# A state-space stage whose time step is computed in another order

## The reference

```
xc, z = split(u @ m_in_w.T)
xc = silu(conv1d(xc) + conv_b)              # 256 channels
x_dbl = xc @ xproj_w.T                      # 8 + 16 + 16 columns
dt = softplus(x_dbl[:, :8] @ dt_w.T + dt_b) # the time step
Bm, Cm = x_dbl[:, 8:24], x_dbl[:, 24:]
# 16 states: h = exp(dt * A) * h + dt * B * u ;  y = sum over states of h * C
y = (y + xc * Dp) * silu(z)
out = y @ m_out_w.T
```

## Time and profile before

| | us |
|---|---|
| median of three timed runs | 2080.14 |
| profiled execution | 2059.48 |
| its span, first to last instruction | 2057.8 |
| TensorE busy | 1652.5 (80%) |
| VectorE busy | 1350.7 (66%) |
| ScalarE busy | 1003.5 (49%) |
| GpSimd busy | 995.8 (48%) |
| mean granted TensorE clock | 0.837 of full |

### The profile page before, as it was taken

One profiled execution on the slowest core, in us unless ns is written; L12 is line 12 of the kernel. 1 busy time (PEld: TensorE's weight loads), 2 busy tenths in 40 slices (PEclk: granted clock), 3 DMA queues, 4 the chain that ended last, 5 costly groups with the idle time before them and its releaser, 6 DMA issues. The chain is left out here.

```text
span 2057.8 us, 23202 instructions
## 1 busy us (share of the span) xinstructions
PE 1652.5 (80%) x7221; PEld 730.4 (35%) x7221; DVE 1350.7 (66%) x1527; ACT 1003.5 (49%) x1638; POOL 995.8 (48%) x524
## 2 busy tenths in 40 slices
PE   7767788888888888875855957698888889879998
PEld 5221222222222222211454744354444445633333
DVE  3079999999999999999552123566565655384444
ACT  3566666676666776674122523154444445441111
POOL 1169999999999999998441153011111000040000
PEclk8878888888888888877957966599999989989999
DMA  3044344434443433333003221422233330100001
GB/s 140 2 104 104 92 103 103 103 93 103 103 103 95 101 90 88 89 87 91 16 30 103 82 67 50 116 59 56 49 77 79 79 79 4 46 0 0 0 0 41
DMA packets 78636, 145.41 MB, mean 71 GB/s; under 512 B 10214, under 2 KB 40782, under 8 KB 76854
## 3 DMA queue, kind: packets, MB, share of 16 engines
q1 hardware_dynamic: 75350, 134.98, 25.8%
q0 software_dynamic: 3216, 9.51, 1.4%
HBM read 87.27 MB, written 23.53 MB: 54 GB/s over the span
## 5 line engine op out<-in xcount | busy, mean ns | idle before, releaser
L574 POOL TENSOR_TENSOR PR<-H,CS 128x1024 f32<-128x1024 f32 x256 | 599.4, 2359 | 75.1 <-DVE H L550 52.8
L550 DVE TENSOR_TENSOR_SCAN H<-DA,X 128x1024 f32<-128x1024 f32 x192 | 431.1, 2273 | 0.0
L456 PE MATMUL psY<-PR,fold 128*64 128x512 f32 x1024 | 341.0, 766 | 4.9 <-POOL PR L574 4.9
L538 DVE TENSOR_TENSOR X<-DU,psB 128x1024 f32<-128x1024 f32 x192 | 235.8, 1228 | 72.9 <-DMA DU<-ab 56.8
L526 ACT ACTIVATE DA<-DT,negA 128x511 f32<-128x511 f32 x384 | 247.6, 709 | 7.3 <-DMA DT<-W 6.4
L1278 ACT ACTIVATE a_PT<-a_psS 128x512 f32<-128x512 f32 x320 | 181.3, 601 | 138.5 <-PE a_psS L1182 134.6
L1325 DVE TENSOR_REDUCE a_MX<-a_psM 128x1 f32<-128x384 f32 (+3 forms) x352 | 205.0, 635 | 47.0 <-PE a_psM L1197 45.5
L1196 PE MATMUL a_psM<-a_kst,a_qst 72*128 72x512 bf16 (+3 forms) x512 | 147.4, 336 | 28.0 <-DMA a_kst<-scratch_k 17.5
L550 DVE TENSOR_TENSOR_SCAN H<-X,XS 128x1024 f32<-128x1024 f32 x64 | 146.2, 2284 | 30.2 <-ACT X L526 30.2
L585 POOL TENSOR_TENSOR XS<-DU,BS 128x1024 f32<-128x1024 f32 x64 | 151.0, 2360 | 0.0
L436 PE MATMUL psB<-ST,sel 96*128 96x512 bf16 x128 | 60.8, 475 | 106.4 <-DVE X L538 106.4
(11 more groups left out here) (258 smaller groups left out, 2733.0 us busy)
## 6 DMA issues: line engine op xcount, KB each, us to landing
CS<-c_rows SPq DMA_DIRECT2D x128, 256.0 KB, 3.8
DT<-W SPq DMA_DIRECT2D x64, 256.0 KB, 4.3
DU<-ab SPq DMA_DIRECT2D x64, 256.0 KB, 4.4
BS<-c_rows SPq DMA_DIRECT2D x64, 256.0 KB, 5.3
scratch_q<-a_partsq SPq DMA_DIRECT2D x24, 384.0 KB, 3.4
a_qst<-scratch_q SPq DMA_DIRECT2D x8, 1152.0 KB
a_kst<-scratch_k SPq DMA_DIRECT2D x24, 384.0 KB
scratch_k<-a_partsk SPq DMA_DIRECT2D x8, 384.0 KB, 4.4
```

Source lines behind the costliest of these rows:

```text
L456: last = nc.tensor.matmul(psY[h * HP:(h + 1) * HP, n % 2 * T:(n % 2 + 1) * T], fold[:, :], chunk(PR[n % 4], h), start=False, stop=n >= NS - 2)
L538: nc.vector.tensor_tensor(both(X[s % 2][:, :]), DU[p][:, at:at + 2, :], psB[:, :].unsqueeze(1).to_broadcast([P, 2, T]), ALU.mult).then_inc ...
L550: nc.vector.tensor_tensor_scan(H[s % 4][:, :], decay, x, 0.0, ALU.mult, ALU.add).then_inc(scan_done, 1)
L574: nc.gpsimd.tensor_tensor(both(PR[s % 4][:, :]), both(H[s % 4][:, :]), CS[q % 2][:, s // 2 % 2, :].unsqueeze(1).to_broadcast([P, 2, T]), A ...
```

## The change

1. In `mamba_inputs_stage` dt's two weights are merged once: TensorE transposes xproj, VectorE copies it, TensorE multiplies its 8 time-step rows with dt_w, VectorE copies the result to dtW (two 128x256 blocks). TensorE does this ahead of its loop.
2. d0 and d1 are each two accumulated 128x128 matmuls of dtW with the activated channels; they no longer need xp and come before it, right behind mout.
3. The sum of softplus' two terms is made by TensorE: s0 and s1 are two identity matmuls each, of rl and ab, and ScalarE copies the result to rl. `pool_dt` is gone.
4. Side steps are placed anew, 12 instead of 10 in a turn; ahead of the loop Silu is split into channels and gate.
5. SP sends DT before it stores the B and C rows, then DU.
6. In attention SP stores the parts before it sends the first half of the maxima.

```diff
+            def _(dve):
+                dve.wait_ge(dtW_step, 1)
+                nc.vector.tensor_copy(xprojT[:, :], dt_ps[0:104, :]).then_inc(dtW_step, 1)
+                dve.wait_ge(dtW_step, 3)
+                nc.vector.tensor_copy(dtW[:, :, :], dtW_ps[:, :, :])
...
+                for c in range(NCH):
+                    last = nc.tensor.transpose(dt_ps[0:104, c * P:(c + 1) * P], w("xproj")[:, c * 104:(c + 1) * 104], w("ident"))
+                last.then_inc(dtW_step, 1)
+                pe.wait_ge(dtW_step, 2)
+                for c in range(NCH):
+                    last = nc.tensor.matmul(dtW_ps[:, c, :], xprojT[96:104, c * P:(c + 1) * P], w("dt_w")[96:104, :], start=True, stop=True)
+                last.then_inc(dtW_step, 1)
...
-        ORDER = ("mout", "xp", "n1", "n2", "d0", "d1", "c0", "c1", "z0", "z1")
-        FIRST = ("c0", "c1", "z0", "z1", "xp", "n1", "n2", "d0", "d1", "c0+", "c1+", "z0+", "z1+")
+        ORDER = ("mout", "d0", "d1", "s0", "s1", "xp", "n1", "n2", "c0", "c1", "z0", "z1")
+        FIRST = ("c0", "c1", "d0", "d1", "s0", "s1", "xp", "n1", "n2", "z0", "z1", "c0+", "c1+", "z0+", "z1+")
...
-        PE_AT = {3: ("mout",), 4: ("xp",), 5: ("n1",), 6: ("n2",), 7: ("d0",), 8: ("d1",),
-                 10: ("c0a",), 11: ("c0b",), 13: ("c1a",), 14: ("c1b",), 16: ("z0",), 17: ("z1",)}
-        ACT_AT = {3: ("silu", "mout"), 4: ("xp",), 5: ("n1",), 6: ("n2",), 7: ("d0",), 8: ("d1",), 12: ("c0",), 15: ("c1",), 16: ("z0",), 17: ("z1",)}
+        PE_AT = {3: ("mout",), 4: ("d0",), 5: ("d1",), 8: ("s0",), 9: ("s1",), 10: ("xp",), 11: ("n1",), 12: ("n2",),
+                 13: ("c0a",), 14: ("c0b",), 15: ("c1a",), 16: ("c1b",), 17: ("z0",), 18: ("z1",)}
+        ACT_AT = {3: ("silu", "mout"), 5: ("d0",), 6: ("d1", "exp"), 7: ("ln",), 8: ("s0",), 9: ("s1",), 10: ("xp",), 11: ("n1",), 12: ("n2",),
+                  14: ("c0",), 16: ("c1",), 17: ("z0",), 18: ("z1",)}
...
-                last = nc.tensor.matmul(pp[:, :], w("dt_w")[96:104, n * P:(n + 1) * P], xd[96:104, :], start=True, stop=True)
+                if k == "d0":
+                    pe.wait_ge(silu_done, v + 2 if u is not None else 1)
+                if k == "s0":
+                    pe.wait_ge(softplus_step, 2 * v + 2)
+                for c in range(NCH):
+                    if k[0] == "d":
+                        last = nc.tensor.matmul(pp[:, :], dtW[:, c, n * P:(n + 1) * P], chunk(UZ[pv], c), start=c == 0, stop=c == NCH - 1)
+                    else:
+                        last = nc.tensor.matmul(pp[:, :], w("ident"), chunk((rl, ab)[c], n), start=c == 0, stop=c == NCH - 1)
...
-        def pool_dt(pool, v, pv):
-            pool.wait_ge(softplus_step, 2 * v + 2)
-            nc.gpsimd.tensor_tensor(rl[:, :], rl[:, :], ab[:, :], ALU.add).then_inc(dtu_ready, 1)
...
-            sp.wait_ge(pp_copied, copied)
-            sp.dma_start(c_rows[ds(v * 2 * NS, 2 * NS), :], xd[0:2 * NS, :]).then_inc(c_stored, 16)
-            sp.wait_ge(dtu_ready, 2 * v + 1)
+            sp.wait_ge(pp_copied, used(u, "s1") + 1)
             spread_halves(sp, rl, DT[pv], dt_loaded)
-            sp.wait_ge(dtu_ready, 2 * v + 2)
+            sp.wait_ge(pp_copied, used(u, "xp") + 1)
+            sp.dma_start(c_rows[ds(v * 2 * NS, 2 * NS), :], xd[:, :]).then_inc(c_stored, 16)
+            sp.wait_ge(dtu_ready, v + 1)
             spread_halves(sp, ab, DU[pv], du_loaded)
...
+                        if c.more_p:
+                            store_parts(sp, c.t + 2, c.p)
                         send_maxima(sp, c.t + 1, 0, c.base + c.use["MA"] + 1, 1 - c.p)
                         if c.more_p:
-                            store_parts(sp, c.t + 2, c.p)
```

More of the change, by code:

```diff
@@ L287, in _, with dt_weights @@
                     (before.pool if before else aside)(pool)
+def dt_weights(W):
+    at = OFF1["wmod0"][0] + NCH * T
+    return W[:, at:at + NCH * NCH * P].rearrange("p (c m) -> p c m", c=NCH)
 def mamba_inputs_stage(nc, W, hT, XP, convW, diagD, sel, fold, nsel):
+    dtW = dt_weights(W)
     w = lambda name: W[:, OFF1[name][0]:OFF1[name][1]]
@@ L295, in mamba_inputs_stage @@
         ps = [ctx.enter_context(nc.psum_tensor(f"xp_ps{i}", [P, T], F32)) for i in range(4)]
+        xprojT = ctx.enter_context(nc.sbuf_tensor("xprojT", [104, NCH * P], F32))
+        dt_ps = ctx.enter_context(nc.psum_tensor("dt_ps", [P, NCH * P], F32))
+        dtW_ps = ctx.enter_context(nc.psum_tensor("dtW_ps", [P, NCH, NCH * P], F32))
         sem = lambda name: ctx.enter_context(nc.semaphore(name))
-        xp_ps_ready, xp_done = sem("xp_ps_ready"), sem("xp_done")
+        xp_ps_ready, xp_done, dtW_step = sem("xp_ps_ready"), sem("xp_done"), sem("dtW_step")
         with nc.Block() as block:
+            @block.vector
+            def _(dve):
[3 more added lines that the diff above has]
+                nc.vector.tensor_copy(dtW[:, :, :], dtW_ps[:, :, :])
             @block.tensor
             def _(pe):
+                for c in range(NCH):
[5 more added lines that the diff above has]
+                last.then_inc(dtW_step, 1)
                 with pe.Fori(0, B // 2) as i:
@@ L347, in mamba_stage @@
         UZ = [sb(f"UZ{i}", [P, 4 * T]) for i in range(2)]
-        xd = W[:, OFF1["wmod0"][0] + NCH * T:OFF1["wmod0"][0] + 3 * T]
+        xd = W[0:2 * NS, OFF1["conv_w"][0]:OFF1["conv_w"][0] + T]
+        dtW = dt_weights(W)
         ST = [sb(f"ST{i}", [96, T], BF16) for i in range(2)]
@@ L417, in pe_step @@
             elif k == "xp":
-                pe.wait_ge(silu_done, v + 1)
                 for c in range(NCH):
@@ L462, in act_step @@
             if k == "silu":
-                act.wait_ge(pp_copied, EACH * u + BEFORE if u is not None else used(None, "z1") + 1)
-                if u is not None:
-                    act.wait_ge(fin_done, u + 1)
+                act.wait_ge(pp_copied, EACH * u + BEFORE)
+                act.wait_ge(fin_done, u + 1)
                 nc.scalar.activation(UZ[pv][:, :], pre[:, :], ACT.Silu).then_inc(silu_done, 1)
+                return
+            if k == "silu_u":
+                act.wait_ge(pp_copied, used(None, "c1") + 1)
+                nc.scalar.activation(UZ[0][:, 0:NCH * T], pre[:, 0:NCH * T], ACT.Silu).then_inc(silu_done, 1)
+                return
+            if k == "silu_z":
+                act.wait_ge(pp_copied, used(None, "z1") + 1)
+                nc.scalar.activation(UZ[0][:, NCH * T:], pre[:, NCH * T:], ACT.Silu).then_inc(silu_done, 1)
+                return
+            if k == "exp":
+                act.wait_ge(pp_copied, used(u, "d1") + 1)
+                nc.scalar.activation(ab[:, :], ab[:, :], ACT.Exp, scale=-1.0).then_inc(softplus_step, 1)
+                return
+            if k == "ln":
+                act.wait_ge(softplus_step, 2 * v + 1)
+                nc.scalar.activation(ab[:, :], ab[:, :], ACT.Ln, bias=1.0).then_inc(softplus_step, 1)
                 return
@@ L475, in act_step @@
                 if u is not None or k.endswith("+"):
-                    act.wait_ge(silu_done, v + 1)
+                    act.wait_ge(silu_done, v + 2)
                 nc.scalar.activation(chunk(pre, n), pp[:, :], ACT.Identity, bias=w("conv_b")[:, n:n + 1]).then_inc(pp_copied, 1)
@@ L485, in act_step @@
                 nc.scalar.copy(ST[pv][0:32, :], pp[0:32, :])
-                nc.scalar.copy(xd[0:104, :], pp[0:104, :]).then_inc(pp_copied, 1)
+                nc.scalar.copy(xd[:, :], pp[0:2 * NS, :]).then_inc(pp_copied, 1)
             elif k[0] == "n":
@@ L489, in act_step @@
                 nc.scalar.copy(ST[pv][rows, :], pp[rows, :]).then_inc(pp_copied, 1)
+            elif k[0] == "s":
+                last = nc.scalar.copy(chunk(rl, int(k[1])), pp[:, :])
+                last.then_inc(pp_copied, 1)
             else:
@@ L496, in act_step @@
                 nc.scalar.activation(chunk(rl, n), pp[:, :], ACT.Relu, bias=w("dt_b")[:, n:n + 1]).then_inc(pp_copied, 1)
[L497 to L501, removed]
         def act_turn(act, u, p, more):
@@ L586, in pool_aside, with pool_du @@
                                     ALU.mult).then_inc(x_ready, 1)
-        def pool_dt(pool, v, pv):
-            pool.wait_ge(softplus_step, 2 * v + 2)
-            nc.gpsimd.tensor_tensor(rl[:, :], rl[:, :], ab[:, :], ALU.add).then_inc(dtu_ready, 1)
-        def pool_du(pool, v, pv):
-            pool.wait_ge(dtu_ready, 2 * v + 1)
+        def pool_du(pool, u, v, pv):
+            pool.wait_ge(pp_copied, used(None if u is None else u, "s1") + 1)
             nc.gpsimd.tensor_tensor(ab[:, :], rl[:, :], UZ[pv][:, 0:NCH * T], ALU.mult).then_inc(dtu_ready, 1)
@@ L605, in pool_turn @@
                     pool_state(pool, 16 * u + j, j - NS, u + 1, 1 - p)
-                if j == 9 and more:
-                    pool_dt(pool, u + 1, 1 - p)
                 if j == 10 and more:
-                    pool_du(pool, u + 1, 1 - p)
+                    pool_du(pool, u, u + 1, 1 - p)
         def spread_halves(sp, source, out, loaded):
```

(41 more changed lines are left out.)

## The result

The changed kernel takes 2158.19 us (median of 4 runs, 2150.04 to 2162.89), the kernel before 2080.76 us beside it. The ratio is 1.0362, with a 95% interval of 1.0321 to 1.0403: slower by 77 us. The forecast was 2152 us, slower.

What follows compares the result with a forecast made beforehand. VectorE, and the order in which TensorE and ScalarE feed it, bound the state-space stage. 90 - 30 + 21 + 1 + 0 + 1 - 10 = +73 us on 2059.5, plus 20.7 for timed runs, gave 2152 us; range 2104 to 2184.

Steps and rivals of the forecast that it cites:

- d0 and d1: State 8's multiply waits because d1, held by d0's late eviction, blocks spread(8): 6.0 us a unit, +90 us.
- State 11: VectorE's wait for state 11's decay disappears because Exp and Ln come earlier: -30 us.
- z0 and z1: At YZ: z0's later eviction delays z1 and psY(15), making YZ late by 1.9 us a unit; +21 us.
- s0 and s1: Before state 12's multiply: spread(12) stands behind s1, 0.5 us a unit; +1 us net, bounds -6 and +46.
- DU: Before the next unit's first multiply: VectorE's wait for DU stays near 0.32 us; 0, bounds -8 and +15.
- Ahead of the loop: Inputs stage and first unit: added work and table loads against a shorter chain; +1 us, bounds -9 and +6.
- Attention: In attention, storing parts earlier frees the load but delays the maxima: 1.75 us earlier an image, -10 us.
- Not held up: Rival: spread and psY matmuls get past the waiting d1 and z1, leaving gains alone; 2030 us, chance 0.08.
- Warm array: Rival: added K=128 work keeps TensorE's clock up at d1; 2118 us, chance 0.24.
- Cold everywhere: Rival: z1 and s0 also run at the slow clock on TensorE; 2184 us and more, chance 0.13.
- Misses its aim: Rival: state 11's decay stays late, so the 30 us come back; 2182 us, chance 0.05.
- attention turns: Rival: in attention the later maxima cost what the earlier load gives; 2162 us, chance 0.08.

Runs made afterwards that it cites:

- d0 early: The changed kernel with d0 and d1 evicted one ScalarE step earlier, ahead of state 7's decay and its wait; ratio 1.0071 to the kernel before.
- run with GpSimd's sum: The mended kernel with softplus' two terms summed by GpSimd again, without s0 and s1; ratio 0.9986 to the kernel before.
- mended kernel: The changed kernel with d0, d1, c1, z0 and z1 handled earlier, spread(12) ahead of s1 and spread(4) ahead of z1; ratio 0.9827, 2041.59 us.
- run with the array kept warm: The changed kernel plus five zero-weight matmuls on TensorE ahead of the waiting d1; ratio 1.0206 to the kernel before.
- first four experiments: Changed kernel with d0 evicted earlier, z0 emptied earlier, or spread(8) ahead of d1; kernel before with only the attention change: 1.0071, 1.0156, 1.0237, 0.9962.
- last four: Changed kernel with d0 and z0 both earlier; then also two spreads earlier; that with GpSimd's sum; changed kernel with zero-weight matmuls: 0.9925, 0.9827, 0.9986, 1.0206.

## Why the prediction was right

- **d0 and d1.** Forecast 15 times 6.0, 90 us, bounds 3.7 and 6.6 each. Measured 89.2 us, 5.4 to 6.8 each; at the fast clock 3.9 to 4.6. The mechanism is the forecast one: d1 waits for d0's eviction, and spread(8) stands behind d1. The slow clock for d1 was right: it was back at 1.00 only at the end of d1 or while psY ran in ten units, and not before psB in five. The forecast gap of 5.2 us is there in ten units (5.15, as at 382.51); in five, as at 322.95, it is 3.55 us, and the clock fell only after d1 had begun.
- **State 11.** Forecast -30; the row is gone.
- **z0 and z1.** Forecast +21; YZ's waits rose by 27.5 us. The single wait was 2.1 us in ten of 14 units and 2.9 to 3.0 in four, for a forecast of 1.9.
- **s0 and s1.** Forecast +1 with bounds -6 and +46. In the changed kernel the wait at state 12 is under 0.5 us. It was hidden by the stall ahead of it: with d0 early it was 1.6 to 1.9 us a unit, 26.9 us. The forecast had the place, but 0.5 us a unit is neither of the two; the price depended on another term, which a sum of separate terms does not show.
- **DU.** Forecast 0; in the loop VectorE's wait fell from 8.5 to 2.2 us, -6, near the lower bound of -8. The run with GpSimd's sum shows that GpSimd's chain to DU is indeed the next bound in the mended kernel.
- **Ahead of the loop.** Forecast +1. The first multiply came 4.8 us earlier, then two waits of 6.70 and 2.46 us for psB followed: +4. I had seen the table loads, not that spread(4) stands behind z0 and z1.
- **Attention.** Forecast -10; the edit alone gave -8 in the timed runs and -10 in its waits, but -3 in the length of its stretch. The forecast had both the earlier load and the later maxima; it had left out the clock behind the new wait.
- **Not held up** (the rival of the other side) is out: matmuls stayed in order in every unit, and moving one of them changed the time. *Warm array* is out for the kernel as it is, but its price was right: the forecast put the time 34 us lower with a warm array, the run with the array kept warm came out 32 us lower. *Cold everywhere* is out: YZ waited 2.1 to 3.0 us and not 3.7, and state 12 under 0.5. *Misses its aim* is out, the wait of state 11 is gone; *attention turns* is out, the edit alone is faster.

The sum of these measured terms is 89 - 30 + 28 - 2 - 6 + 4 - 10 = +73 us (psB's other waits in the loop fell by about 2), as forecast; the timed medians differ by 77. The main cost and the 30 us back are right by themselves. That the sum is right to the microsecond is luck: the smaller terms are off by +7, -3, -6 and +3 us. The 2152 also holds 20.7 us, the distance between the profiled execution and the timed runs, for which the forecast had no cause.

## What to carry to other kernels

Where engines take their work in program order, place a step by what is queued behind its waits on both engines: here one eviction behind one semaphore wait cost 89 us of waits, and one step earlier 6 us. Follow the chain past the first wait removed; each repair uncovered the next queue (state 8, then state 12, then DU). An idle gap ahead of a critical matmul was paid twice here, by the gap and by the slow clock after it (3.12 to 3.78 us for d1 instead of 1.99).

## What was not expected of the hardware

Matmuls with all-zero weights kept the granted clock at 1.00 through the gap, and adding them made the kernel 32 us faster.

In the kernel before, the 2.55 us gap at 304.43 was followed by some 13 us at the lower clock, although TensorE was busy without a break, 2.00 us of 2 in each window from 306 to 318. One of them:

```profile
310.00:312.00 2.00, 2.00 (x4) 0.60 (x3) 1.90 (x2) 1.42 (x3) 1.00 (x2) 0.50 0.07 12
```

In the changed kernel the clock was back some 6 us after d1 began, at the latest. Why the one stretch is twice the other was not tried.

The profiled execution of the changed kernel lost some 20 us in a stage that no edit touches (third row of the table). Of VectorE's idle times there the first ended with ScalarE, which was late itself, and the others have no releaser that the profile knows:

```profile
1316.05 0.18 DVE L276 RECIPROCAL ln_rs<-ln_sd 128x4 f32<-128x4 f32 x1 [7.37 <-ACT ln_sd L258]
1325.60 0.75 DVE L1090 SCALAR_TENSOR_TENSOR xT<-gps,mod,xT 128x512 f32<-128x512 f32 x1 [9.36 <-issue]
1330.48 0.69 DVE L272 COPY work<-ln_xc 128x512 f32<-128x512 f32 x1 [4.14 <-remote]
```

It is no accident of one execution. The same stretch took 332 to 342 us in the traces of the first four experiments, on the chip where the kernel before had a median of 2060.2 us, and 349 to 356 us in those of the last four, where it had 2078.9. The trace of the kernel before is of the short kind (335.9 us) although its timed runs gave 2080. So the stretch goes with the chip or the occasion, not with the change; its 20.2 us can account for the traces being 90.6 us apart and the medians 77, and it may be most of the 20.7 us that the forecast added without a cause. Neither was shown. What it is stays open. A forecast in absolute time holds only for its chip.
